# GpSimd drains in front of every second gather in layer 3 of a graph network kernel

## The reference

```python
weights, idx = _spline_basis(edge_attr)          # 3 attributes: 8 weights per edge
B = zeros(Etot, 8).at[arange(Etot)[:, None], idx].add(weights)
xj = x[src]
z = (B[:, :, None] * xj[:, None, :]).reshape(Etot, S * 64)
msg = z @ W.reshape(S * 64, 64)
agg = segment_sum(msg, dst, num_segments=6250)
out = agg / maximum(cnt, 1.0)[:, None] + x @ root
# batch norm over the nodes, elu; then layernorm(x + ...)
```

## Time and profile before

| | us |
|---|---|
| median of 3 runs | 10398.82 (10390.36 to 10400.64) |
| the profiled execution, first to last instruction (span) | 11537.7 |
| gathers of layer 3 in it, first to last start | 9037.5 to 11326.8 |
| busy in it: VectorE, GpSimd, ScalarE, TensorE | 6821.8, 6567.8, 4714.2, 3146.5 |

### The profile page before, as it was taken

How to read it: one execution, slowest core, us unless ns; L and a number is a source line. 1 busy time by engine, 2 the same in 40 slices (tenths; PEclk the granted TensorE clock), 3 DMA queues, 4 the chain that set the end, 5 groups by cost and what they waited for, 6 DMA issues and landing times. The chain is left out here.

```text
span 11537.7 us, 92744 instructions
## 1 busy us (share of the span) xinstructions
PE 3146.5 (27%) x19432; PEld 2586.9 (22%) x19432; DVE 6821.8 (59%) x9436; ACT 4714.2 (41%) x6523; POOL 6567.8 (57%) x6626
## 2 busy tenths in 40 slices
PE   1111588882000000000023555555554200000002
PEld 1111477772000000000013444444443100000001
DVE  6777666664222311159962777777775566666664
ACT  1111466661211111137731666666662343334342
POOL 5656666665677777730023666666662466666663
PEclk9999767675555555555555677776775655555555
DMA  3332322222333323235522444444441666666662
GB/s 91 88 83 78 80 60 71 71 82 26 121 112 111 107 94 106 103 125 207 205 104 52 117 118 124 117 116 122 118 117 39 194 202 201 199 202 205 203 201 70
DMA packets 722783, 1395.92 MB, mean 121 GB/s; under 512 B 409552, under 2 KB 439453, under 8 KB 715095
## 3 DMA queue, kind: packets, MB, share of 16 engines
q0 software_dynamic: 287072, 587.19, 19.4%
q1 hardware_dynamic: 406786, 639.32, 17.0%
q10 hardware_dynamic: 28852, 168.65, 4.0%
HBM read 827.48 MB, written 602.51 MB: 124 GB/s over the span
## 5 line engine op out<-in xcount | busy, mean ns | idle before, releaser
L822 POOL DMA_INDIRECT l_rows<-in_x,l_idx x1568 | 1613.7, 1029 | 1010.1 <-issue 431.0
L2445 POOL DMA_INDIRECT l_rows<-table,l_idx x1568 | 1487.5, 949 | 1032.2 <-issue 483.2
L1925 POOL DMA_INDIRECT l_rows<-h,l_idx x1568 | 1540.3, 982 | 882.1 <-issue 442.4
L1303 POOL DMA_INDIRECT rows<-l_rows,l_idx x1568 | 1548.9, 988 | 554.0 <-issue 526.3
L1960 PE MATMUL l_made<-l_kv_w,l_rows_t 128*128 128x256 f32 x3136 | 1117.3, 514 | 1041.1 <-ACT l_kv L1990 402.5
L1960 PEld LDWEIGHTS l_made<-l_kv_w,l_rows_t 128*128 128x128 f32 x3136 | 761.2, 259 | 1279.5 <-issue 1147.1
L2521 ACT ACTIVATE l_lifted<-l_rows,l_up 128x256 f32<-128x256 f32 x1568 | 653.2, 463 | 824.0 <-DVE l_half_low L2473 527.1
L1698 PE MATMUL l_wide<-l_diag,l_ones 128*128 128x384 f32 x4 | 3.3, 926 | 3218.0 <-DVEq L1728 3218.0
L1259 ACT COPY l_rows<-l_run 128x1792 f32<-128x1792 f32 x56 | 191.6, 3421 | 1636.1 <-POOLq L88 1359.5
L1292 DVE TENSOR_TENSOR l_rows<-l_run,l_weights_ps 128x56 f32<-128x56 f32 x56 | 12.0, 215 | 1371.0 <-POOLq L88 1168.7
L1698 PEld LDWEIGHTS l_wide<-l_diag,l_ones 128*128 128x128 f32 x4 | 1.0, 312 | 3218.9 <-DVEq L1728 3218.9
(11 more groups left out here) (393 smaller groups left out, 12672.9 us busy)
## 6 DMA issues: line engine op xcount, KB each, us to landing
sums<-l1s_out ACTq DMA_DIRECT2D x56, 1988.0 KB, 7.1
sums<-l_out SPq DMA_DIRECT2D x112, 924.0 KB
spread<-zeros SPq DMA_DIRECT2D x28, 3612.0 KB
l_spread<-spread SPq DMA_DIRECT2D x112, 903.0 KB
l1s_rows<-rows SPq DMA_DIRECT2D x56, 1008.0 KB, 4.7
spread<-zeros SPq DMA_DIRECT2D x56, 938.0 KB
l_spread<-spread SPq DMA_DIRECT2D x56, 938.0 KB
sums<-l_out ACTq DMA_DIRECT2D x56, 896.0 KB
```

What stands on the lines that cost most here:

```text
L822: pool.indirect_dma_start(rows[:, b, t], None, a["x"], bass.IndirectOffsetOnAxis(ap=idx[:, b, t:t + 1], axis=0)) \
L1303: pool.indirect_dma_start(g["rows1_d"], bass.IndirectOffsetOnAxis(ap=idx[:, b, t:t + 1], axis=0), rows[:, b, t], None).then_inc(sent[b], 16)
L1925: pool.indirect_dma_start(rows[:, c.r, t, 0:C], None, g["h2_d"], bass.IndirectOffsetOnAxis(ap=idx[:, c.r, t:t + 1], axis=0)).then_inc(got[ ...
L2445: pool.indirect_dma_start(rows[:, b, t], None, g["table3_d"], bass.IndirectOffsetOnAxis(ap=idx[:, b, t:t + 1], axis=0)) \
```

## The change

In front of the gathers at t = 2, 4, 6, 10, 12 and 14 of each chunk GpSimd now executes a drain. At t = 0 and 8 stands the wait as before. No other line is changed, and the order of all other instructions on all engines is the same; lines below the change have numbers higher by two.

```diff
                         for t in range(T):
                             if t % HALF == 0:
                                 wait(pool, rows_used[b][t // HALF], h + 1)
+                            elif t % 2 == 0:
+                                pool.drain()
                             pool.indirect_dma_start(rows[:, b, t], None, g["table3_d"],
                                                     bass.IndirectOffsetOnAxis(ap=idx[:, b, t:t + 1], axis=0)) \
                                 .then_inc(got[b][t // HALF], 16)
```

## The result

| | before | after |
|---|---|---|
| median of 4 runs, us | 10394.66 | 12376.78 (12344.73 to 12398.87) |
| ratio | | 1.191, 95% interval 1.189 to 1.193 |
| profiled span, us | 11537.7 | 12342.9 |

The change makes the kernel slower by 1982 us, 19%. The forecast was 10611. One thing must be said to read the numbers: the kernel before has two levels, about 10390 us in some sessions and about 11790 us in others, in every execution of a session.

The account below looks back on a forecast made before the run. In a run, layer 3's chunk was taken to be bound by GpSimd's 20.0 us against VectorE's 16.7. Six drains per chunk at 0.36 us add 2.16 us, over 98 chunks 212: 10398.8 + 212 = 10611 us, range 10380 to 10787.

Parts of the forecast that it names:

- VectorE's gaps: Layer 3's loop: idle stretches behind VectorE's drains with no releaser, 506 us in the traced stretch, 5.9 us per chunk.
- the missing 1139 us: Whole kernel: runs were 1139 us shorter than the profiled execution; GpSimd's gather-loop waits, 1338 us, were taken to shrink in runs.
- x = 0.36 us: Price per added drain on GpSimd: held start 0.66 us less the present gap of 0.30; 212 us in all.
- the upper bound, 0.66 us: Highest price per added drain: GpSimd's whole start path added to the present 0.30 us gap; 388 us for 588.
- the range to 10787: Forecast range for the runs, 10380 to 10787 us; it left out the landing case and most of the faster one.
- the 2.86 us of the landing: Loop start: time from a chunk's last gather ending to the start of the lift that needs its half.
- The run-ahead: GpSimd's sequencer prepares the next gather while one is worked on; a drain takes that away, 0.36 us each.
- The start path behind a release: GpSimd: time from a held gather's release to its start, about 0.66 us.
- The rival with the landing: Each added drain waits until gathered rows have landed: 2.56 x 588 = 1505 us more, 11900 us; chance 0.05.
- The rival with the bouts: Drains on GpSimd break up VectorE's bouts of long gaps: 118 us less, 10281 us; chance 0.12.
- The profile's forecast: Profiled span would hardly move: 2.16 us per chunk go into GpSimd's 3.4 us of waiting, with VectorE's stalls unchanged.

Follow-up runs that it names:

- the second trace of before: The kernel before, unedited, traced again: 10397 us in its one run; layer 3's loop took 1964.5 us, 20.0 per chunk.
- the no-operations: 588 sequencer no-operations in place of the changed kernel's drains: 10388 against 10389 us for before, 1.0003; 1.0004 at the higher level.
- the single drains: Changed kernel with one drain per chunk, at t = 4, 98 in all: 10764 against 10389 us for before; 1.0033 and 1.0039 at the higher level.

## Why the prediction was wrong

- **What bounds a run: right.** GpSimd with 20.0 us per chunk; the second trace of before shows it, and the no-operations and the single drains behaved as it says.
- **Why the trace had more: wrong.** I put VectorE's gaps down to the recording. They are a level of the kernel that goes with the session: 42 runs of before in two sessions lie between 11739 and 11860 us. Whether it is the chip is not shown, as no chip was used in two of these sessions. The inference from the missing 1139 us hit the bound and missed its cause, and a recorded execution at the lower level would have refuted it.
- **The step that failed** is "A drain holds every later instruction of GpSimd until the gather before it has finished on the engine". It holds them until the rows have landed: all 588 drains end 0.12 us or more after the landing. From the false step came x = 0.36 us; measured 3.41 us of GpSimd's time each, and 1982 us for 212. Even the upper bound, 0.66 us, rested on it, so the range to 10787 could not hold the time.
- **The rows that I bounded by were the wrong kind.** VectorE's drain stands behind work of VectorE alone. GpSimd's last instruction had a DMA in flight, and the near row for that was the 2.86 us of the landing. I had it, and gave it 0.05 on the ground that gathers are released one by one without waiting to land. That says nothing of a drain, since gathers are also released without waiting for each other.
- **The run-ahead: not the term I made of it.** That the sequencer works ahead fits the free no-operations. The start path behind a release, read as 0.66 us, was nearly right: 0.70 us from each drain's end to the next gather. But it comes on top of the landing instead of being the whole.
- **The rival with the landing** was the right one and said 11900. It missed 477 us. Its 2.86 us for the landing was good (the mean in the changed kernel is 2.85 from a gather's end), but it left out what follows the landing, the drain's end and the start path: 0.86 us on the mean, 588 x 0.86 = 506, near the 477.
- **The rival with the bouts** pointed at something real: at the higher level VectorE's gaps are gone when GpSimd pauses in every chunk. Its price for a pause, 0.36 us against 3.4 to 4.2, was off by the same step; it needed a price under 0.56 us to gain anything.
- **The profile's forecast** ("the span would hardly move"): wrong for the same step.

## What to carry to other kernels

A drain on GpSimd behind gathers of its own is a wait for their landing: price it by the trace's time from issue to landing plus the engine's start path, not by another engine's drain. Other engines that issue DMAs were not tried. Where GpSimd is the one that bounds the loop, the full price is paid each time; elsewhere only what exceeds its waiting. If it must have the wait, a wait on the gathers' own semaphore costs slightly less than the drain. And before a gap in a trace is explained, compare the span with the runs: where they differ by over a per cent, take a second trace of the same kernel first.

## What the runs showed of the hardware that I had not expected

- A drain on GpSimd waits for landing: mean gaps of 3.18, 3.71 and 4.21 us with a drain in front of nearly every gather, of every second and of one in 16, at 256 KB per gather, and 2.31 in front of every second at 32 KB. It ends 0.07 us after the landing with one gather since the last drain and 0.69 us with 16, and the next gather starts 0.70 us after that.
- The Trainium skill, DMA: Bandwidth & Descriptors (Anatomy of one DMA — SWDGE (gpsimd) path), gives a fit of 2.0 us plus bytes at 436 GB/s for a DMA of this path. By that an estimate for the two sizes is 2.6 and 2.1 us; the trace has 3.5 and 2.4 from a gather's start to its landing, so the measured landing is what counts here.
- A gather costs GpSimd 1.25 us for 256-byte rows as for 2 KB rows (10400 against 10389 us for the whole kernel).
- The same kernel took 10.39 ms in some sessions and 11.79 ms in others. At the higher level VectorE has gaps of up to 5.2 us behind its drains, in bouts, also with small rows, when the DMA engines are busy for 0.16 instead of 0.67. With one pause of GpSimd per 24 us they were gone; what causes them was not found.
